# Token embedding of a ViT tower kernel: position rows as three 16-bit parts, tiles 2 to 4 from 16-bit halves, first loads in thirds, and another order of sums on GpSimd

## What is computed

```
h = patches @ W.T + b ; class token in front ; + pos_embedding     # 32 x 37 rows of 256
x = layernorm(h)                                                   # no weights
x = x + attn(ln1(x)) @ o_w.T + o_b         # q, k = elu + 1, sum over the 16 heads of one token
x = x + gelu(ln2(x) @ fc_w.T + fc_b) @ proj_w.T + proj_b
h = h + x
y = layernorm(h) ; out = h + moe(y) + shared(y)    # 16 experts, each takes its 148 best tokens
```

## Time and profile before

| | |
|---|---|
| median of 3 runs | 476.94 us (476.86 to 477.66) |
| the profiled execution, its own time | 477.49 us |
| its span, first to last instruction | 475.7 us |
| mean granted clock of PE | 0.986 of full |
| PE, DVE, ACT, POOL busy | 437.1, 344.8, 261.3, 191.2 us |

### The profile page before, as it was taken

How to read it: one execution, slowest core, us unless ns; L and a number is a source line. 1 busy time by engine, 2 the same in 40 slices (tenths; PEclk the granted TensorE clock), 3 DMA queues, 4 the chain that set the end, 5 groups by cost and what they waited for, 6 DMA issues and landing times.

```text
span 475.7 us, 10747 instructions
## 1 busy us (share of the span) xinstructions
PE 437.1 (92%) x4019; PEld 386.8 (81%) x4019; DVE 344.8 (72%) x614; ACT 261.3 (55%) x663; POOL 191.2 (40%) x233
## 2 busy tenths in 40 slices
PE   6899999988988997998997999899999999999990
PEld 3578788867977887886776889799999999999980
DVE  1099998899889899013898895888777777776620
ACT  1566576877786876374520044655565666555520
POOL 1329356357337332121000441664543644444432
PEclk9999999999999998999999999999999999999995
DMA  6723392000000000000000059788888888888321
GB/s 248 268 71 105 97 429 87 14 12 0 12 13 0 12 12 12 2 16 18 9 0 1 7 158 395 282 314 301 285 311 318 318 315 316 316 298 293 103 29 14
DMA packets 17350, 69.14 MB, mean 145 GB/s; under 512 B 4338, under 2 KB 10399, under 8 KB 12834
## 3 DMA queue, kind: packets, MB, share of 16 engines
q1 hardware_dynamic: 12130, 61.96, 35.0%
q0 software_dynamic: 4608, 5.41, 5.6%
q10 hardware_dynamic: 576, 1.29, 0.7%
HBM read 63.32 MB, written 5.33 MB: 144 GB/s over the span
## 4 chain that ended last, share of the span: by engine, by line
PE 51%; DVE 7%; issue 3%; POOL 3%; DMA 3%; ACT 2%; ACTq 0%; POOLq 0%; DVEq 0%
PE bank L1471 18%; PE bank L1482 13%; PE bank L1267 4%; PE bank L1238 4%; DMA wex_s<-in_wex 3%; PE bank L1225 3%; PE bank L1252 2%; PE bank L1378 2%; DVE wproj_s L997 2%; DVE scratch L1014 2%; PE bank L1493 1%; POOL rstd L434 1%; PE bank L1449 1%; POOL tmp L432 1%; DVE late L1066 1%
## 5 line engine op out<-in xcount | busy, mean ns | idle before, releaser
L533 POOL DMA_INDIRECT out_rows<-scratch,slot_s x32 | 53.9, 1684 | 84.2 <-DMA out_rows<-scratch,slot_s 63.8
L1482 PE MATMUL bank<-scratch,wex_s 128*128 128x148 f32 x512 | 77.7, 295 | 0.5 <-DVE scratch L1106 0.5
L522 POOL DMA_INDIRECT xg<-token_rows,slot_g x32 | 41.2, 1286 | 70.5 <-DVE slot_g L1079 61.6
L1482 PEld LDWEIGHTS bank<-scratch,wex_s 128*128 128x128 f32 x512 | 67.6, 190 | 1.0 <-DVE scratch L1106 1.0
L813 ACT ACTIVATE scratch<-bank 128x296 f32<-128x296 f32 x64 | 26.6, 416 | 66.6 <-PE bank L1471 66.6
L1471 PE MATMUL bank<-scratch,wfc_s 128*128 128x148 f16 x512 | 52.6, 227 | 0.3 <-DVE wproj_s L997 0.3
L1471 PE MATMUL bank<-scratch,wsh_s 128*128 128x148 f16 x512 | 52.7, 227 | 0.0
L432 POOL TENSOR_SCALAR tmp<-spread 128x1 f32<-128x1 f32 x30 | 19.5, 650 | 80.1 <-ACT beside L588 40.3
L1471 PE MATMUL bank<-scratch,wproj_s 128*128 128x148 f16 x256 | 50.6, 227 | 0.0
L997 DVE SCALAR_TENSOR_TENSOR wproj_s<-wex_s,wfc_s 128x512 f16<-128x512 f32 x64 | 40.4, 682 | 12.5 <-ACT wfc_s L796 12.5
L1106 DVE SCALAR_TENSOR_TENSOR scratch<-bank,scratch 128x296 f32<-128x296 f32 x64 | 29.4, 460 | 26.5 <-ACT scratch L813 26.3
(11 more groups left out here) (175 smaller groups left out, 943.7 us busy)
## 6 DMA issues: line engine op xcount, KB each, us to landing
wex_s<-in_wex SPq DMA_DIRECT2D x16, 2048.0 KB
wex_s<-in_wex SPq DMA_DIRECT2D x16, 1024.0 KB, 8.3
patch_s<-in_patches SPq DMA_DIRECT2D x10, 384.0 KB
token_rows<-y_s SPq DMA_DIRECT2D x10, 128.0 KB, 1.7
out_rows<-h_all SPq DMA_DIRECT2D x5, 256.0 KB, 6.6
wex_s<-in_wfc SPq DMA_DIRECT2D x1, 1024.0 KB, 5.2
...
```

The source lines that it names most:

```text
L522: gp.indirect_dma_start(xg[b][:], None, rows, bass.IndirectOffsetOnAxis(slot_g[b][:], 0))\
L533: gp.indirect_dma_start(out, bass.IndirectOffsetOnAxis(slot_s[b][:], 0), eo[b], None, compute_op=ALU.add).then_inc(scattered, 16)
L1482: last = pe.matmul(ps_down[k][:, 0:C], wex_s[s.par][:, lo:lo + P], hexT[:, m, :], start=(m == 0), stop=(m == MC - 1))
```

## The change

1. **Position rows.** `base_s` is split by DVE into three bfloat16 parts, which DMAs stack into one 117-row operand `base16`; the selector becomes a bfloat16 matrix `sel16` for all tiles, loaded once in two pieces. One bfloat16 matmul takes the place of the float32 one in every tile. For tile 0 it comes last, not first.
2. **Tiles 2 to 4.** ACT converts `wtok_s` in three pieces and the patches of tiles 2, 3, 4 to float16 upper halves, DVE makes the lower halves. Each of these tiles is embedded by 18 float16 matmuls in place of six float32 ones. The halves lie in `wex_s`, so SP waits for all ten embeddings before it loads expert 1.
3. **Loads.** The weights and patch of tile 0 come in thirds on both queues, tile 1's patch in two halves; of `consts` only the identity comes early. Patches 2 to 4 are loaded early into `wex_s`.
4. **First chain.** Tile 0's reciprocal roots are shared out between DVE and POOL (`first_shift`), q and k are projected before v, and the filler matmuls go from 8 to 3.
5. **POOL.** `rest_of_x2` is called ahead of `sum_hx` and `norm_f` in each turn.

```diff
-            sp.dma_start(wtok_s[:], wtok).then_inc(w_in["tok"], 16)
-            load_patch(Step(0, 0))
             sp.dma_start(base_s[:], base).then_inc(w_in["tok"], 16)
+            sp.dma_start(wtok_s[:, third(0), :], wtok[:, third(0), :]).then_inc(first_in[0], 16)
+            sp.dma_start(patch_s[0][:, third(1), :], patches[0, :, third(1), :]).then_inc(first_in[1], 16)
+            sp.dma_start(wtok_s[:, third(2), :], wtok[:, third(2), :]).then_inc(first_in[2], 16)
+            sp.dma_start(sel16[:, 0:2 * P], marks[:, 0:2 * P]).then_inc(marks_in[0], 16)
+            sp.dma_start(patch_s[1][:, 0:half, :], patches[1, :, 0:half, :]).then_inc(patch_in[1], 16)
+            sp.wait_ge(base_made, 5)
+            for q in range(1, 3):
+                sp.dma_start(base16[q * BASE:(q + 1) * BASE, :], base_part[:, q, :]).then_inc(base_in, 16)
             sp.wait_ge(bias_made, 5)
             sp.dma_start(parts.rearrange("n (p j) -> p n j", p=P), bpart[:]).then_inc(bias_out, 16)
-            load_patch(Step(0, 1))
-            sp.wait_ge(ones_made, 1)
+            sp.dma_start(raw_patch[2], patches[2]).then_inc(raw_in[2], 16)
+            sp.dma_start(sel16[:, 2 * P:TP], marks[:, 2 * P:TP]).then_inc(marks_in[1], 16)
+            sp.dma_start(kst[:, K_TRI:KCOLS], consts[:, K_TRI:KCOLS]).then_inc(rest_in, 16)
...
+            sp.wait_ge(tok_done, TILES)
             load_gu(Step(0, 1), 1)
...
-            norm_a(Step(0, 0), after(5))
+            gp.wait_ge(var_made, 1)
+            gp.tensor_tensor(rstd[:, 0:1], tmp[:, 0:1], nhalf[:], ALU.pow).then_inc(root_made, 1)
+            gp.wait_ge(var_made, 2)
+            gp.tensor_tensor(rstd[:, 3:4], tmp[:, 5:6], nhalf[:], ALU.pow).then_inc(a_rstd, 1)
...
                 if t >= 2:
+                    rest_of_x2(s.off(-2))
                     sum_hx(s.off(-2))
                 if t >= 3:
                     norm_f(s.off(-3), after(2))
-                if t >= 2:
-                    rest_of_x2(s.off(-2))
...
+            for c in range(3):
+                dst, src = (wtok_s, wtok) if c == 1 else (patch_s[0], patches[0])
+                act.dma_start(dst[:, c * CHUNK:(c + 1) * CHUNK, :], src[:, c * CHUNK:(c + 1) * CHUNK, :])\
+                   .then_inc(patch_in[0] if c == 2 else first_in[c], 16)
...
+            halve_tok()
             act.wait_ge(w_in["consts"], 32)
             act.activation(col2[:], colc[:, COL_LN2W:COL_LN2W + 2 * KC], ACT.Copy, scale=XSPLIT).then_inc(col2_made, 1)
             copy_h(Step(0, 0))
+            halve_patch(2)
             norm_a(Step(0, 0))
             scale_xh(Step(0, 0))
+            turn_xn(Step(0, 0))
             copy_h(Step(0, 1))
-            turn_xn(Step(0, 0))
-            copy_v(Step(0, 0))
+            halve_patch(3)
+            halve_patch(4)
             negate_qk(Step(0, 0))
             exp_qk(Step(0, 0))
+            copy_v(Step(0, 0))
...
+            rest_of_tok()
+            first_shift()
+            for t in SPLIT_TILES:
+                rest_of_patch(t)
...
-                pe.matmul(ps_tok(t)[:, 0:D], sel_s[s.par][:], base_s[:], start=True, stop=False)
+                pe.matmul(ps_tok(t)[:, 0:D], sel16[:, t * P:(t + 1) * P], base16, start=True, stop=False)
+                if t in SPLIT_TILES:
+                    pe.wait_ge(plo_made, t - 1)
+                    products = [(patch16[t][b][:, k, :], wtok16[a][:, k, :]) for b, a in ((0, 0), (0, 1), (1, 0)) for k in range(TKC)]
```

142 lines of the change are left out of this document (118 added, 24 removed).

## The result

| | before | after |
|---|---|---|
| median (lowest to highest, 4 runs each) | 476.90 us (476.82 to 477.66) | 469.45 us (468.19 to 469.65) |
| the profiled execution | 477.49 us | 468.19 us |
| its span | 475.7 us | 466.2 us |
| mean granted clock of PE | 0.986 | 0.980 |

The ratio after to before is 0.9838, 95% interval 0.9807 to 0.9869: faster by 7.5 us, where 13.7 were forecast. The forecast time was 463.3 us and its range ended at 469.0, so the result lies 0.45 us outside. The profiled execution of the kernel after (468.19) is the fastest of its four and lies inside; the other three took 469.4 to 469.7.

What follows compares the result with a forecast made beforehand. Bounds: DVE's wait for tile 0's chain in the start, then turns of 16.86 us set by PE and ACT, just above DVE's 15.62. Terms 4.1 + 0.3 + 2.6 + 4.9 + 0.5 + 1.3 = 13.7 us, median 463.3, range 459.0 to 469.0.

Steps and rivals of the forecast that it cites:

- The start: Start up to DVE's first `combine`: that row at 19.4 instead of 23.50 us, gain 4.1, bounds 1.0 and 5.5.
- the landing of the base parts: In the start: issued about 6.67 us or a little earlier, landing 1.7 to 3.7 us later, at 8.1 to 10.1.
- tile 2's patch: Start, before `xh`: its conversion (about 0.87 us) lies in the wait for the roots; otherwise costs up to 0.9.
- the bias rows: Start, before `combine`: small bias loads standing behind the 4 MB asked for would give the lower bound, gain 1.0.
- rival A: Start gives little: a small DMA behind other loads ends last, `combine` about 22.5, gain 1.0, time 466.4; chance 15%.
- Turns 0 and 1: POOL's `rest_of_fc` still takes port time from DVE's products; gain 0.3 us, bounds -1 and 3.15.
- Turn 3: Cheaper embeddings save PE 5.9 us in turns 0 to 2, felt in turn 3: gain 2.6, bounds 0 and 2.8.
- POOL's order: Turns 4 to 7: PE's 1.55 us wait for x2 goes, gain 4.9; turn 8: `hx` waits behind x2, gain 0.5.
- B: Turns stay where they are, with 0.3 us more in `expo`'s chain: gain 2 instead of 4.9, time 467.8; chance 13%.
- D: Slower: PE's clock falls once in each of nine turns, 14.7 us against 13.7, time 478; chance 3%.
- Turn 9 and behind: From turn 9 PE sets the end: gain 1.3 us, bounds 0.5 and 3; what follows the turns shifts as a whole.
- rival C: More than the sum: POOL's port time and turn 9's low clock (1.63 us) go as well, time 458.8; chance 10%.

Runs made afterwards that it cites:

- e1: The changed kernel run again with no edit; median 468.21 us, ratio to before 0.9796.
- e15: The changed kernel without 16-bit halves, base rows loaded stacked three times in one load instead of copied; median 465.36 us, ratio to before 0.9735.
- e16: The changed kernel with its halves, base rows loaded stacked three times in one load instead of copied; median 468.47 us, ratio to before 0.9812.
- e10: The changed kernel without 16-bit halves, tiles 2 to 4 embedded from float32; median 465.02 us, ratio to before 0.9737.
- e11: e10 with four more thrown-away 16-bit base products in each embedding from tile 1 on; median 468.98 us, ratio to before 0.9791.
- e8: The kernel before with only POOL's new order added; median 472.92 us, ratio to before 0.9922.
- e7: The changed kernel with POOL's old order put back; median 475.30 us, ratio to before 0.9954.

## Why the prediction was wrong, and where it was right

**The start (4.1 us; measured 0.65, and 1.55 in e1).** This is the step that failed. Its beginning held: six products ended at 8.56, and ACT was through at 9.6, 0.5 us late because `colc` came at 9.37. The term that broke is the landing of the base parts, "1.7 us (a small store) to 3.7", at 8.1 to 10.1: the second copy, issued at about 5.3, landed at 11.5, after 6.2 us. Those rows were measured in other company, 1.7 with empty queues, 3.7 with nearly 4 us of loads still to come; the change asks for three patches (1.15 MB) more in the same microseconds. The two further links, tile 2's patch "if it is there" and the bias rows, were named and then set at nothing. The patch came at 14.3 and the bias parts at 13.5 (13.1 in e1), and e15 and e16 show that they would have held the chain even with the copies away. The lower bound of this term (1.0) and rival A described the mechanism, and A's `combine` at 22.5 lies between the 22.85 and 21.95 of the two profiles; the measured 0.65 lies below even that bound.

**Turns 0 and 1 (0.3; -0.5).** The halving of `wfc` came earlier, as the prediction said, but POOL's two operations (33.27 to 39.78) then lay on both products with v (4.03 and 4.23 us), and no longer on q*k. The text had drawn a time 0.9 lower from the rule on the shared port in the Trainium skill (SBUF — State Buffer, "SBUF: two separate sides"), by which one of the two operations would lie free beside DVE's sums. The sums were over at 32.44, so neither did: the 1.22 in turn 1 went, but 1.74 came in turn 0. The rule was not at fault, its use was, and the difference of the two is the -0.5.

**Turn 3 (2.6; 2.60).** The number is right, and so is the mechanism, saved PE time that is used in turn 3. Its account was not: the sum counted 5.9 us of PE time, 3.3 of it in the three 16-bit tiles (of which the halves themselves save 1.9, 2.13 us instead of 2.75 in each), and e10 shows that the position rows suffice (15.93), e11 that they are needed (19.17). The margin was thin: `norm_f` ends 0.06 us before DVE's products, and e8 and e11 lose 3.23 us where it doesn't. The sum did not know of this, so that the number is exact is in part luck. It also took POOL's order as an edit apart; without the rows the order makes this turn 2.1 us longer (e8).

**POOL's order (4.9 and 0.5; 5.26 and 0.54).** Right, with its mechanism: e7 and e8 show 16.85 and 15.54 both ways. PE and ACT were fast enough, DVE's 15.54 is the bound. Rivals B and D are out: no slice of turns 1 to 8 is below the full clock.

**Turn 9 and behind (1.3; 2.35 and then -1.34).** "I let it shift as a whole" is the second step that failed. The low clock of turn 9 went, which gave the 1.63 us that only rival C had; without it 0.7 is left of the 1.3. But this was luck of one execution and no work of the change: in e1 the clock falls in turn 9 again, with the same waits in front (1.49 and 0.36 us, against 1.50 and 0.35), and the row takes 4.04 us. The same loss came back behind the search: 40 down products take 10.42 us where they took 8.74. Nothing in the diff touches that place.

With the measured start the sum would have been 13.7 - 3.45 = 10.25, and with the measured turns 0 and 1 as well 9.44. The errors of the other stages nearly cancel (9.30 measured); from there to 7.45 it is the 1.85 us by which the two profiled executions stand off their medians. What the halves cost was in the sum, 0.9 us in front of `neg` and up to 0.9 in front of `x_all`; what it missed is that nothing stands against it, since the PE time that they save in turns 0 to 2 is not needed.
